# Expert outputs of the second layer's first step: four groups summed on VectorE, and the token sums as one fp32r pass

## The chip, the cores and the metric

The kernel runs on one core of one Trainium2 chip. The metric is device time in microseconds (us). One execution also has a hardware profile; its rows are what this document reads. The engines are TensorE (PE, with its weight loads as PEld), VectorE (DVE), ScalarE (ACT), GpSimd (POOL) and the queue of SyncE (SPq), which issues most DMAs.

## The reference

Two layers over 8 batches of 512 tokens and 256 channels. The part that matters is the hand-over between them: the mixture of 32 experts of the first layer is added back to the tokens, and this sum opens the second layer.

```python
# first layer, experts choose tokens (b = 8, E = 32, K = 8, s = 512)
vals_t, idx_t = jax.lax.top_k(probs.transpose(0, 2, 1), K)
...
h = jax.nn.gelu(h, approximate=False)
o = jnp.einsum('bej,ejo->beo', jnp.concatenate([h, ones], -1), w2)
out_tok = jnp.einsum('beo,bke->bkeo', o, vals).reshape(b, K * E, d)
out = jnp.zeros_like(x).at[jnp.arange(b)[:, None], flat_idx].add(out_tok)
...
x = x + _L0_attn_ref(xn, ...) + _L0_ffn_ref(xn, ...)
xn = _layernorm(x, axis=-1)
x = x + _L1_attn_ref(xn, ...) + _L1_ffn_ref(xn, ...)
```

The scatter-add is written as a matrix product. For a batch, `pick` (32 experts x 512 tokens) holds the weight with which an expert's output goes to a token, and `out = pick^T o`.

## The kernel before

`attend` is the first layer. It runs NTURN = 64 turns (8 batches x 8 head pairs), and beside the attention it computes one of the 32 experts every two turns. An expert's hidden units are cut into GRP = 4 groups, and each group's share of the output stays apart: the DRAM tensor `eo_d` holds, for each expert, 4 x 32 rows (group, batch slot) of 256 channels. `second_layer` follows in the same program. It holds one function for each engine, and each engine works through its own instructions in the order in which they are written; semaphores (`Signal`) tie the engines together, and `wait_ge` holds back everything behind it on its engine.

The tensor instructions of the second layer run as `first()` for batch 0, then `turn(b)` for b = 0 to 6, then `last(7)`. `turn(b)` does the products of batch b and, between them, the opening steps of batch b + 1:

- `add(b+1)` (L1547): the token sums. Four matmuls 128x128 by 128x256, plain fp32, write the added expert outputs of 512 tokens into the banks `bF`. All four groups are in the contraction: the 128 rows of `pick4` are `pick` four times over, and the 128 rows of `eo` are 4 groups x 32 experts. Each fp32 matmul has two records in the trace.
- `memory(b)`, `up(b, ...)` (L1581, L1600), `down(b, ...)` (L1611, L1617): the products of batch b, all of them pairs of high and low fp32r parts (hi x lo, lo x hi, hi x hi).
- `turn_x(b+1)` (L1557) transposes the normalised tokens, `router(b+1)` (L1565) and `turn_shut(b+1)` (L1572) do the routing of the second layer.

In `first()` the order is `add(0)`, two quarters of the last output projection of the first layer (`output`, L972), `turn_x(0)`, a third quarter, `router(0)`, the fourth quarter, `turn_shut(0)`. `add(0)` stands right behind the last `values` (L928) of the first layer.

On VectorE `front(0)` opens the second layer: `norm(0)` adds the residual to the banks (L1707), takes the statistics (L1712, L1715, L1717), waits for GpSimd's power (L1698) and writes the normalised tokens (L1721); later come `split`, `choose` and `copy_shut` (L1760). What stands ahead of it on VectorE is the last low part of the attention output, `yT_lo` (L1297). In `turn(b)` the order ends with `copy_shut(b+1)` and `finish(b)` (L1776, two halves, one for each half of `down`), and the next turn begins with `norm`.

On SyncE `get_x` loads the tokens and four copies of `pick` (L1514, L1516), `get_eo` the expert outputs (L1520); both for batch b + 2 as soon as `add` and the residual sum of batch b + 1 are done (`free`). The tiles `eo` and `pick4` have one buffer each.

```python
for j in range(GRP):
    eng.dma_start(eo[j * E:(j + 1) * E, :], eo_d[:, j * E + b, :]).then_inc(load.sem, load.unit)
...
def add(b):
    eng.wait_ge(load.sem, load.at(b))
    eng.wait_ge(lo_done.sem, lo_done.at(b - 1))
    eng.wait_ge(shutT_done.sem, shutT_done.at(b - 1))
```

Of the kernel before, what the change touches and what calls it, by code (L numbers as in the profile page):

```python
# [7 lines left out]
F32 = mybir.dt.float32  # L8
F32R = mybir.dt.float32r
# [591 lines left out]
def attend(nc, t, out, g):  # L601
# [18 lines left out]
    with ExitStack() as ctx:  # L620
# [10 lines left out]
        qkn = sq  # L631
        slope32 = sb("slope32", [P, NT, 2])
        shift32 = sb("shift32", [P, NT, 2])
        qT_hi, qT_lo = sb("qT_hi", [P, T], F32R), sb("qT_lo", [P, T], F32R)
        kT_hi, kT_lo = sb("kT_hi", [P, T], F32R), sb("kT_lo", [P, T], F32R)
        routed, scores, hidden, early = share(
            nc, ctx, "area_p", routing_tiles(g),
            tuple((f"prob{u}{h}", [P, off[NT]], F32) for u in range(2) for h in range(2)) + (
# [100 lines left out]
        def filled(n):  # L739
# [5 lines left out]
        jobs_at.update({(NTURN, 0): (8, 9), (NTURN, 1): (10, 11)})  # L745

        second = second_layer(nc, t, out, dict(
            g, ctx=ctx, up_hi=up_hi, up_lo=up_lo, downT_hi=downT_hi, downT_lo=downT_lo, readT_hi=readT_hi, readT_lo=readT_lo,
            spread=spread, shutT=shutT, rT=rT, number=number, area_raw=area_raw, area_sq=area_sq, hidden=hidden,
            hT=hidden["hT"], area_w1=area_w1, area_w2=area_w2, bF=bS[1:3], bR=bS[0], bU=bQ, bD=bR[0:2], bMem=bR[2],  # L750
            x1_stored=xr_store, prepared=prepared))
# [1 line left out]
        with nc.Block() as block:  # L753
            @block.sync
            def _(eng):
                def load_xT(b):
                    eng.wait_ge(pe_q.sem, pe_q.at((b - 1) * HP - 1))
                    eng.dma_start(xT_hi[:, b % 2, :, :].bitcast(F32), xnT_hi_d[b]).then_inc(xT_load[b % 2].sem, 16)
                    eng.dma_start(xT_lo[:, b % 2, :, :].bitcast(F32), xnT_lo_d[b]).then_inc(xT_load[b % 2].sem, 16)

                def load_w1(m):
                    eng.wait_ge(pe_h.sem, pe_h.at(m - 1))
                    eng.dma_start(w1[:, :, :], t["L0_ffn_w1"][m, 0:C, :].rearrange("(k p) f -> p k f", p=P)).then_inc(w1_load.sem, 16)
                    eng.wait_ge(biased.sem, biased.at(m - 1))
                    for j in range(GRP):
                        eng.dma_start(bias1[j * E:(j + 1) * E, :], t["L0_ffn_w1"][m, C, j * FW:(j + 1) * FW].partition_broadcast(E)).then_inc(
                            bias1_load.sem, 16)

                def load_w2(m):
                    eng.wait_ge(pe_eo.sem, pe_eo.at(m - 1))  # L770
                    eng.dma_start(w2[:, :, :], t["L0_ffn_w2"][m, 0:F, :].rearrange("(j p) c -> p j c", p=P)).then_inc(w2_load.sem, 16)
                    eng.wait_ge(eo_done.sem, eo_done.at(m - 1))
                    eng.dma_start(bias2[0:E, :], t["L0_ffn_w2"][m, F, :].partition_broadcast(E)).then_inc(bias2_load.sem, 16)

                def store_eo(m):
                    eng.wait_ge(eo_done.sem, eo_done.at(m))
                    eng.dma_start(eo_d[m], eo).then_inc(eo_store.sem, 16)
                route.sync(eng)
                route.over(eng)
                load_w1(0)  # L780
                load_w2(0)
                eng.dma_start(proj_in[:, :, :], t["L0_attn_Wproj"].rearrange("(h p) c -> p h c", p=P)).then_inc(wp_load.sem, 16)
                eng.dma_start(g["rb"][:], t["L1_ffn_router_b"].partition_broadcast(P)).then_inc(g["l1_load"], 16)
                eng.dma_start(g["backT"][g["M1"]:g["M1"] + 1, :], t["L1_ffn_b2"].unsqueeze(0)).then_inc(g["l1_load"], 16)
                with nc.allow_non_contiguous_dma(reason="1024 biases, once"):
                    eng.dma_start(g["b1"][:, :], t["L1_ffn_b1"].rearrange("(h p) -> p h", p=P)).then_inc(g["l1_load"], 16)

                for s in range(NTURN + 1):
                    b = s // HP
                    if begins_in(s) is not None and begins_in(s) + 1 < E:  # L790
                        load_w1(begins_in(s) + 1)
                    if s % HP == 1:
                        eng.wait_ge(xr_store.sem, xr_store.at(b - 1))
                        eng.dma_start(xr[:, :, :], t["L0_attn_x"][b].rearrange("(n p) c -> p n c", p=P)).then_inc(xr_load.sem, 16)
                    if s % HP == HP - 2 and b + 2 < B:
                        load_xT(b + 2)
                    if s == NTURN - 1:
                        eng.wait_ge(squared.sem, squared.at(s))
                        eng.wait_ge(norm_done.sem, norm_done.at(s))
                        eng.wait_ge(gate_in.sem, gate_in.at(s))  # L800
                        eng.wait_ge(v_done.sem, v_done.at(s))
                        second.get_x(eng, 0)
                    if s == NTURN - HP - 1:
                        eng.wait_ge(pe_q.sem, pe_q.at(NTURN - HP - 1))
                        for i in range(2):
                            eng.dma_start(w1n[i][:, :, :], t["L1_ffn_w1"][i * 4 * P:(i + 1) * 4 * P, :].rearrange(
                                "(h p) c -> p h c", p=P)).then_inc(w1n_load.sem, 16)
                    if s == NTURN - 2:
                        eng.wait_ge(pe_h.sem, pe_h.at(E - 1))
                        eng.dma_start(w2n[:, :, :], t["L1_ffn_w2"].rearrange("(k p) f -> p k f", p=P)).then_inc(w2n_load.sem, 16)  # L810
                    if ends_in(s) is not None:
                        store_eo(ends_in(s))
                        if ends_in(s) + 1 < E:
                            load_w2(ends_in(s) + 1)
                    if s == NTURN - 1:
                        eng.wait_ge(pe_eo.sem, pe_eo.at(E - 1))
                        for dst, src in ((rn, t["L1_ffn_router_w"]), (m1n, t["L1_attn_W1"]),
                                         (m2n[:, :, :], t["L1_attn_W2"].rearrange("(k p) m -> p k m", p=P)),
                                         (wk[:, :, :], t["L1_attn_W_K"].rearrange("(k p) c -> p k c", p=P))):
                            eng.dma_start(dst, src).then_inc(small_load.sem, 16)  # L820
                    if s > 0 and s % HP == 0:
                        if s == NTURN:
                            eng.wait_ge(eo_store.sem, eo_store.at(E - 1))
                            second.get_eo(eng, 0)
                            second.free(eng, 0)
                            second.get_x(eng, 1)
                            second.get_eo(eng, 1)
                        eng.wait_ge(o_done.sem, o_done.at(b - 1))
                        eng.dma_start(x1_d[b - 1].rearrange("(n p) c -> p n c", p=P), xr[:, :, :]).then_inc(xr_store.sem, 16)
                eng.wait_ge(g["l1_load"], 3 * 16)  # L830
                second.sync(eng)
# [626 lines left out]
def second_layer(nc, t, out, g):  # L1458
# [13 lines left out]
    xo = area[:, N:2 * N].rearrange("p (n c) -> p n c", n=NT)  # L1472
    pick4 = area[:, 2 * N:2 * N + T]
    eo = area[:, 2 * N + T:2 * N + T + C]
    area = g["area_w1"]
    x1 = area[:, :].rearrange("p (u n c) -> p u n c", u=2, n=NT)
    area = g["area_w2"]
# [19 lines left out]
    shut = piece(NT * NB).rearrange("p (n i) -> p n i", n=NT)  # L1497

    ev = lambda name, per, unit=1: Signal(ctx, nc, name, per, unit)
    load, store = ev("load3", 2 * GRP + 1, 16), ev("store3", 1, 16)  # L1500
    pe_add, pe_xT, pe_r, pe_shut = ev("pe_add", 2), ev("pe_xT3", 2), ev("pe_r", 1), ev("pe_shut", 1)
    pe_mem, pe_up, pe_down = ev("pe_mem", 1), ev("pe_up", HC), ev("pe_down", 2)
# [14 lines left out]

    def get_eo(eng, b):
        for j in range(GRP):
            eng.dma_start(eo[j * E:(j + 1) * E, :], eo_d[:, j * E + b, :]).then_inc(load.sem, load.unit)  # L1520

    def free(eng, b):
        eng.wait_ge(pe_add.sem, pe_add.at(b))
# [16 lines left out]
    def tensor(eng, output):  # L1540

        def add(b):
            eng.wait_ge(load.sem, load.at(b))
            eng.wait_ge(lo_done.sem, lo_done.at(b - 1))
            eng.wait_ge(shutT_done.sem, shutT_done.at(b - 1))
            for n in range(NT):
                m = eng.matmul(bF[n // 2][:, (n % 2) * C:(n % 2 + 1) * C], pick4[:, n * P:(n + 1) * P], eo[:, :],  # L1547
                               start=True, stop=True)
                if n % 2:
                    m.then_inc(pe_add.sem, pe_add.unit)  # L1550
# [102 lines left out]

    def scalar(eng):

        def copy_x(b):
            eng.wait_ge(hi_done.sem, hi_done.at(b - 1))
            eng.wait_ge(lo_done.sem, lo_done.at(b - 1))
# [17 lines left out]
        def turn(b):  # L1676
            memory(b)
            relu(b, range(0, 3))
            copy_x(b + 1)
            relu(b, range(3, HC))  # L1680

        def last(b):
            memory(b)
            relu(b, range(HC))
        copy_x(0)
        for b in range(B - 1):
            turn(b)
        last(B - 1)
# [9 lines left out]
            eng.tensor_tensor(rstd[:, :], var[:, :], half[:, 0:NT], ALU.pow).then_inc(rstd_done.sem, rstd_done.unit)  # L1698

    def vector(eng, output):  # L1700

        def norm(b):
            eng.wait_ge(load.sem, load.at(b))
# [74 lines left out]
                    x1[:, b % 2, 2 * i:2 * i + 2, :], ALU.add).then_inc(out_done.sem, out_done.unit)  # L1778

        def front(b):  # L1780
            norm(b)
            output(0)
            output(1)
# [2 lines left out]
            choose(b)  # L1786
            output(3)
            copy_shut(b)

        def turn(b):  # L1790
            norm(b + 1)
# [3 lines left out]
            choose(b + 1)  # L1795
            relu_low(b, range(6, HC))
            copy_shut(b + 1)
            finish(b)

        def last(b):  # L1800
# [29 lines left out]
```

## Time and profile before

| what | value |
|---|---|
| median of 3 runs | 1371.68 us (1370.08 to 1376.79) |
| the profiled execution's own time | 1374.09 us |
| its span in the profile | 1372.4 us |
| mean granted TensorE clock | 0.983 of full speed |
| PE busy | 1321.2 us, 96% of the span |
| DVE busy | 1057.4 us, 77% |
| ACT busy | 938.2 us, 68% |
| POOL busy | 194.8 us, 14% |
| second layer (first `add` to the last output) | 1097.7 to about 1372 us |

Times of rows are microseconds from the start of the span, unless a row says ns. The profiled execution took 1.7 us more than its span, and 2.4 us more than the median. "PEclk" in rows is the clock that TensorE was granted, as a share of its full 2.4 GHz; 0.50 is 1.2 GHz.

### The profile page before, as it was taken

Reading aid. Unit: us, or ns where it says so; the run is one execution under the profiler, and the core shown is the slowest. Engines: PE = TensorE matmul, PEld = TensorE weight load, DVE = VectorE, ACT = ScalarE, POOL = GpSimd, SP = SyncE. Lnnn points to the kernel's source line nnn. Section 1 sums busy time; section 2 is a strip of 40 time slices with the busy share of each in tenths; the row PEclk is TensorE's granted clock in tenths of the full one; section 3 lists DMA queues with packets and bytes.
Section 4 is the critical chain, followed back from the end, with each engine's and each line's share of the span. In section 5 each row is a group of like instructions: output and inputs, shape, how many; then the busy total and the mean of one; then the engine's idle time right before and its main releaser. Section 6 shows DMA issues by size and latency. Waiting matters only on the chain.

```text
span 1372.4 us, 31987 instructions
## 1 busy us (share of the span) xinstructions
PE 1321.2 (96%) x11472; PEld 1114.1 (81%) x11472; DVE 1057.4 (77%) x3292; ACT 938.2 (68%) x2357; POOL 194.8 (14%) x564
## 2 busy tenths in 40 slices
PE   4989999999999999999999999999999799999998
PEld 2678888888888888888888888878887588999897
DVE  6869996999699699969996996999699665544542
ACT  5759885888588588858886895988588433333333
POOL 4612111111011111111110111111111100000000
PEclk8699999999999999999999999999999899999999
DMA  5552241323233232413232332223132221111100
GB/s 209 189 167 87 73 136 54 119 101 100 73 102 107 75 98 74 134 57 117 101 106 67 106 103 83 91 83 126 65 109 67 79 70 43 43 43 43 43 16 31
DMA packets 88335, 123.15 MB, mean 90 GB/s; under 512 B 8577, under 2 KB 74482, under 8 KB 88178
## 3 DMA queue, kind: packets, MB, share of 16 engines
q1 hardware_dynamic: 87858, 121.11, 27.6%
q8 instruction: 92, 1.51, 0.5%
q14 instruction: 65, 0.53, 0.1%
q10 hardware_dynamic: 320, 0.00, 0.0%
HBM read 101.69 MB, written 19.40 MB: 88 GB/s over the span
## 4 chain that ended last, share of the span: by engine, by line
PE 76%; ACT 13%; DVE 4%; issue 2%; DMA 0%; POOL 0%; SPq 0%; ACTq 0%; DVEq 0%; POOLq 0%
PE at L848 15%; PE at L861 9%; PE at L900 8%; PE at L928 8%; PE at L1581 7%; PE at L972 7%; PE at L1617 7%; ACT prob L1114 5%; PE at L881 2%; PE at L939 2%; PE at L892 2%; ACT probT L1123 1%; PE at L886 1%; ACT area_raw L1071 1%; ACT L1133 1%
## 5 line engine op out<-in xcount | busy, mean ns | idle before, releaser
L1114 ACT ACTIVATE prob<-prob,low 128x512 f32<-128x512 f32 (+3 forms) x512 | 280.8, 551 | 115.9 <-DVE low L1268 115.9
L1268 DVE CUSTOM_DVE_ANT_0 prob<-at,mask 128x512 f32<-128x512 f32 (+3 forms) x512 | 219.8, 485 | 9.8 <-PE at L861 9.8
L848 PE MATMUL at<-w_hi,c_lo 128*128 128x386 f32 x512 | 189.9, 371 | 1.5 <-DVE area_raw L1213 1.5
L848 PE MATMUL at<-w_lo,c_hi 128*128 128x386 f32 x512 | 174.0, 340 | 0.0
L848 PE MATMUL at<-w_hi,c_hi 128*128 128x386 f32 x512 | 173.8, 340 | 0.0
L1281 DVE TENSOR_SCALAR prob<-prob,rec 128x512 f32<-128x512 f32 (+3 forms) x512 | 169.4, 395 | 4.5
L900 PE MATMUL at<-ident,prob 128*128 128x128 f32 x1280 | 165.6, 276 | 3.1 <-DVE low L1268 1.8
L928 PE MATMUL at<-probT,v 128*32 128x512 f32 (+3 forms) x2048 | 152.9, 439 | 4.6 <-DVE probT L1291 2.8
L900 PEld LDWEIGHTS at<-ident,prob 128*128 128x128 f32 x1280 | 143.5, 142 | 10.6 <-DVE yT_lo L1297 1.6
L928 PEld LDWEIGHTS at<-probT,v 128*32 128x32 f32 x2048 | 68.2, 110 | 90.5 <-issue 81.8
L1123 ACT ACTIVATE probT<-at 128x512 f32<-128x512 f32 (+1 forms) x256 | 130.3, 536 | 5.3 <-PE at L900 2.7
L1401 POOL TENSOR_TENSOR slope<-gl,omega 128x8 f32<-128x8 f32 x64 | 12.8, 200 | 836.7 <-DVE gl L1242 836.7
L1071 ACT ACTIVATE area_raw<-at 128x386 f32<-128x386 f32 x192 | 93.5, 487 | 19.8 <-PE at L848 18.1
L848 PEld LDWEIGHTS at<-w_hi,c_lo 128*128 128x128 f32 x512 | 97.0, 189 | 2.2 <-DVE area_raw L1213 1.9
L848 PEld LDWEIGHTS at<-w_lo,c_hi 128*128 128x128 f32 x512 | 97.3, 190 | 0.0
L1114 ACT ACTIVATION_READ_ACCUMULATOR prob<-prob,low 128x1 f32 x512 | 96.8, 189 | 0.0
L848 PEld LDWEIGHTS at<-w_hi,c_hi 128*128 128x128 f32 x512 | 96.7, 189 | 0.1
L861 PE MATMUL at<-kT_hi,qT_hi 64*128 64x512 f32 (+3 forms) x512 | 86.5, 332 | 6.6 <-ACT kT_hi L1101 6.6
L861 PE MATMUL at<-kT_lo,qT_hi 64*128 64x512 f32 (+3 forms) x512 | 84.9, 325 | 1.5
L861 PE MATMUL at<-kT_hi,qT_lo 64*128 64x512 f32 (+3 forms) x512 | 84.6, 324 | 0.0
L1667 ACT ACTIVATE mem<-at 64x512 f32<-64x512 f32 x8 | 4.8, 594 | 116.0 <-PE at L1581 116.0
L861 PE MATMUL at<-kaug,qaug 64*128 64x512 f32 (+3 forms) x512 | 83.2, 319 | 0.0
(225 smaller groups left out, 3243.5 us busy)
## 6 DMA issues: line engine op xcount, KB each, us to landing
area_w<-in_L_ffn_w SPq DMA_DIRECT2D x65, 1024.0 KB, 5.7
bias<-in_L_ffn_w SPq DMA_DIRECT2D x160, 32.0 KB, 4.5
x_in<-in_L_attn_x SPq DMA_DIRECT2D x8, 512.0 KB, 5.5
xr<-in_L_attn_x SPq DMA_DIRECT2D x8, 512.0 KB, 4.9
eo_d<-hidT SPq DMA_DIRECT2D x32, 128.0 KB, 1.8
x_d<-xr SPq DMA_DIRECT2D x8, 512.0 KB, 3.0
area_raw<-x_d SPq DMA_DIRECT2D x8, 512.0 KB, 3.9
out<-area_raw SPq DMA_DIRECT2D x8, 512.0 KB, 2.9
```

Of the source, the lines that this page charges most:

```text
L848: m = eng.matmul(bQ[n % 2][:, 0:W], a[:, (j // HP) % 2, k, n * P:(n + 1) * P], w[:, k, j % HP, :], start=start, stop=(k == KC - 1 and a is ...
L861: m = eng.matmul(bC[i][:, at:at + (c + 1) * P], q[rows, c * P:(c + 1) * P], k[rows, 0:(c + 1) * P], start=ready is k_hi_done, stop=q is qaug)
L900: m = eng.transpose(bP[h][i][:, at:at + P], prob[s % 2][h][:, off[c] + kc * P:off[c] + (kc + 1) * P], ident[:, :])
L928: m = eng.matmul(bY[rows, kc * P:T], v[:, s % 2, kc, rows], probT[j * E // D][:, offT[kc]:offT[kc + 1]], start=(kc == 0), stop=(kc == NT - 1))
L972: m = eng.matmul(bQ[n % 2][:, 0:C], y[:, h, n * P:(n + 1) * P], w[:, h, :], start=(h == 0 and y is yT_lo), stop=(h == HP - 1 and y is yT_h ...
L1071: eng.activation(raw[:, j % 2, n, :], bQ[n % 2][:, 0:W], ACT.Copy).then_inc(raw_A.sem, 1)
L1114: eng.activation(sl, sl, ACT.Exp, scale=-1.0, bias=low[:, i:i + 1], accum_out=den[:, i:i + 1]).then_inc(exp_done.sem, 1)
L1123: eng.activation(probT[h][:, x:y], bP[h][i][:, 0:y - x], ACT.Copy).then_inc(done.sem, 1)
L1268: eng.tensor_tensor_reduce(out=prob[s % 2][h][:, off[c]:off[c + 1]], in0=bC[i][:, at:at + (c + 1) * P], in1=mask[:, (NT - 1 - c) * P:T], s ...
L1281: p = eng.tensor_scalar(sl, sl, rec[:, k:k + 1], None, ALU.mult)
L1581: m = eng.matmul(bank[:, :], w[:, k, :], x[:, b % 2, k, :], start=start, stop=(k == KC - 1 and w is hi and x is xT_hi))
L1617: m = eng.matmul(o, part[:, h, n * P:(n + 1) * P], w[:, h, :], start=False, stop=(h == HC - 1 and part is hT_hi and w is downT_hi))
```

## The change

The four groups are no longer summed by the contraction. `get_eo` loads all four groups of every expert into each of four blocks of 32 rows (a new tile `eo4`, 128 x 4 x 256), and a reduction on VectorE sums them, so that every block holds the same 32 summed outputs. The contraction's 128 rows then carry the high and low parts instead: `eo_s` is high, low, high, low by blocks of 32 rows, and `pick_s` is high, high, low, low. One fp32r matmul over 128 rows gives all four partial products. ScalarE rounds `pick4` to its high part (`high_pick`), VectorE does the reduction and the rest (`split_eo`). The new tiles lie over `qT_hi`, `qT_lo`, `kT_hi` and `kT_lo` of the first layer, for which SyncE waits for the last scores before its first `get_eo`.

```diff
@@ attend
-        qT_hi, qT_lo = sb("qT_hi", [P, T], F32R), sb("qT_lo", [P, T], F32R)
-        kT_hi, kT_lo = sb("kT_hi", [P, T], F32R), sb("kT_lo", [P, T], F32R)
+        turned, added = share(
+            nc, ctx, "area_q", tuple((n, [P, T], F32R) for n in ("qT_hi", "qT_lo", "kT_hi", "kT_lo")),
+            (("eo4", [P, GRP, C], F32), ("pick_s", [P, T], F32R), ("eo_s", [P, C], F32R)))
...
                         if s == NTURN:
                             eng.wait_ge(eo_store.sem, eo_store.at(E - 1))
+                            eng.wait_ge(pe_s.sem, pe_s.at(NTURN - 1))
                             second.get_eo(eng, 0)
...
     def get_eo(eng, b):
         for j in range(GRP):
-            eng.dma_start(eo[j * E:(j + 1) * E, :], eo_d[:, j * E + b, :]).then_inc(load.sem, load.unit)
+            eng.dma_start(eo4[j * E:(j + 1) * E, :, :], eo_d.rearrange("e (j i) c -> i e j c", j=GRP)[b]).then_inc(load.sem, load.unit)
...
         def add(b):
-            eng.wait_ge(load.sem, load.at(b))
+            eng.wait_ge(eo_split.sem, eo_split.at(b))
...
-                m = eng.matmul(bF[n // 2][:, (n % 2) * C:(n % 2 + 1) * C], pick4[:, n * P:(n + 1) * P], eo[:, :],
+                m = eng.matmul(bF[n // 2][:, (n % 2) * C:(n % 2 + 1) * C], pick_s[:, n * P:(n + 1) * P], eo_s[:, :],
                                start=True, stop=True)
...
     def scalar(eng):
+        def high_pick(b):
+            eng.wait_ge(load.sem, load.at(b))
+            eng.wait_ge(pe_add.sem, pe_add.at(b - 1))
+            eng.activation(pick_s[:, :], pick4[:, :], ACT.Copy).then_inc(pick_hi.sem, pick_hi.unit)
...
             relu(b, range(3, HC))
+            if b + 2 < B:
+                high_pick(b + 2)
...
+        high_pick(0)
         copy_x(0)
+        high_pick(1)
...
     def vector(eng, output):
+        def split_eo(b):
+            eng.wait_ge(load.sem, load.at(b))
+            eng.wait_ge(pe_add.sem, pe_add.at(b - 1))
+            eng.tensor_reduce(eo[:, :], eo4[:, :, :].rearrange("p j c -> p c j"), AX.X, ALU.add).then_inc(eo_sum.sem, eo_sum.unit)
+            eng.wait_ge(eo_sum.sem, eo_sum.at(b))
+            eng.tensor_copy(eo_s[:, :], eo[:, :]).then_inc(eo_hi.sem, eo_hi.unit)
+            eng.wait_ge(eo_hi.sem, eo_hi.at(b))
+            for j in (1, 3):
+                rows = slice(j * E, (j + 1) * E)
+                eng.tensor_tensor(eo_s[rows, :], eo[rows, :], eo_s[rows, :].bitcast(F32), ALU.subtract).then_inc(eo_split.sem, eo_split.unit)
+            eng.wait_ge(pick_hi.sem, pick_hi.at(b))
+            eng.tensor_tensor(pick_s[2 * E:P, :], pick4[2 * E:P, :], pick_s[2 * E:P, :].bitcast(F32), ALU.subtract).then_inc(
+                eo_split.sem, eo_split.unit)
...
         def front(b):
+            split_eo(b)
             norm(b)
...
             copy_shut(b)
+            split_eo(b + 1)
 
         def turn(b):
...
             copy_shut(b + 1)
+            if b + 2 < B:
+                split_eo(b + 2)
             finish(b)
```

VectorE's order where the second layer begins, before (`area_w<-at,area_raw` is the residual sum of `norm`, the tiles of the second layer are slices of `area_raw`, `area_w` and `area_sq`):

```order
L1291 COPY probT<-at 128x384
L1297 TENSOR_TENSOR yT_lo<-at,yT_hi 128x512
L1707 TENSOR_TENSOR area_w<-at,area_raw 128x512 x2
L1712 BN_STATS area_sq<-area_w 128x6 x4
L1715 BN_AGGR area_sq<-area_sq 128x2 x4
L1717 TENSOR_SCALAR area_sq<-area_sq 128x4
L1721 TENSOR_SCALAR area_w<-area_w,area_sq 128x256 x4
```

The same place after the change, with batch 0's reduction (`eo` is `eo4`, `area_raw` here the summed outputs, then `pick4`):

```order
L1294 COPY probT<-at 128x384
L1300 TENSOR_TENSOR yT_lo<-at,yT_hi 128x512
L1719 TENSOR_REDUCE area_raw<-eo 128x256
L1721 CAST eo_s<-area_raw 128x256
L1725 TENSOR_TENSOR eo_s<-area_raw,eo_s 32x256 x2
L1727 TENSOR_TENSOR pick_s<-area_raw,pick_s 64x512
L1735 TENSOR_TENSOR area_w<-at,area_raw 128x512 x2
L1740 BN_STATS area_sq<-area_w 128x6 x4
```

Five instructions stand between the last `yT_lo` of the first layer and the first `norm`; batch 1's five stand in the same way between `copy_shut(0)` and `norm(1)`.

VectorE's order at the end of a turn, before (`shutT` is `copy_shut`, `area_raw<-at,area_w` the two halves of `finish`):

```order
L1755 TENSOR_SCALAR area_sq<-area_sq 128x64
L1769 TENSOR_TENSOR hT_lo<-hT,hT_hi 128x512 x2
L1760 CAST shutT<-at 16x512
L1776 TENSOR_TENSOR area_raw<-at,area_w 128x512 x2
L1707 TENSOR_TENSOR area_w<-at,area_raw 128x512 x2
L1712 BN_STATS area_sq<-area_w 128x6 x4
```

The same place after the change:

```order
L1783 TENSOR_SCALAR area_sq<-area_sq 128x64
L1797 TENSOR_TENSOR hT_lo<-hT,hT_hi 128x512 x2
L1788 CAST shutT<-at 16x512
L1719 TENSOR_REDUCE area_raw<-eo 128x256
L1721 CAST eo_s<-area_raw 128x256
L1725 TENSOR_TENSOR eo_s<-area_raw,eo_s 32x256 x2
L1727 TENSOR_TENSOR pick_s<-area_raw,pick_s 64x512
L1804 TENSOR_TENSOR area_raw<-at,area_w 128x512 x2
L1735 TENSOR_TENSOR area_w<-at,area_raw 128x512 x2
```

In turns 0 to 5 the five instructions of batch b + 2 stand between `copy_shut(b+1)` and `finish(b)`. On TensorE nothing moves; its eight `add` have four records each instead of eight.

## Rows read from the trace of the kernel before

**Rows 1.** The page, busy time of each engine over the span.

```profile
PE 1321.2 (96%) x11472; PEld 1114.1 (81%) x11472; DVE 1057.4 (77%) x3292; ACT 938.2 (68%) x2357; POOL 194.8 (14%) x564
```

**Rows 2.** Stretches: each engine's busy us, then PEclk, DMA share, GB/s.

```profile
1115.20:1147.50 32.30, 32.30 (x203) 28.97 (x204) 15.72 (x44) 11.72 (x19) 1.01 (x1) 1.00 0.15 45
```

**Rows 3.** The chain that ended last, one turn: start us, us, what.

```profile
1147.57 1.73 PE at L1547 x8
...
1176.94 2.84 PE at L1617 x24
1179.78 1.73 PE at L1547 x8
```

**Rows 4.** The same chain where the second layer begins.

```profile
1097.78 1.92 PE at L1547 x8
1099.70 5.67 PE at L972 x48
...
1113.78 0.52 PE at L1572 x4
1114.33 0.69 DVE shutT L1760
1115.15 1.97 PE at L1547 x8
```

**Rows 5.** VectorE in order of time, there: start, us, what, [idle before].

```profile
1098.63 0.69 DVE L1297 TENSOR_TENSOR yT_lo<-at,yT_hi 128x512 fp32r<-128x512 f32 x1 [5.64 <-ACT yT_hi L1128]
1099.24 1.28 DVE L1707 TENSOR_TENSOR area_w<-at,area_raw 128x512 f32<-128x512 f32 x2
```

**Rows 6.** VectorE's groups by shape: count, busy us, mean ns, idle before.

```profile
L1217 DVE TENSOR_REDUCE ssq<-area_sq 128x16 f32<-128x1024 f32 x64 | 77.8, 1215 | 4.8 <-ACT area_sq L1078 4.8
...
L1769 DVE TENSOR_TENSOR hT_lo<-hT,hT_hi 128x512 fp32r<-128x512 f32 x64 | 44.2, 691 | 35.4 <-ACT hT_hi L1674 34.4
...
L1313 DVE TENSOR_TENSOR hidT<-at,bias 128x256 f32<-128x256 f32 x32 | 13.4, 418 | 4.0 <-PE at L956 4.0
...
L1727 DVE CAST c_hi<-area_w 128x1024 fp32r<-128x1024 f32 x8 | 5.6, 694 | 2.7 <-ACT area_w L1662 2.7
```

**Rows 7.** DMA: first loads of the experts' outputs on SyncE's queue.

```profile
1084.35 1.85 SPq L1520 DMA_DIRECT2D area_raw<-eo_d  x4
1100.59 0.38 SPq L1514 DMA_DIRECT2D area_raw<-x_d  x1
```

**Rows 8.** The page, DMA issues: count, KB each, median us to landing.

```profile
area_raw<-x_d SPq DMA_DIRECT2D x8, 512.0 KB, 3.9
```

**Rows 9.** Stretches around two idle times of TensorE; columns of Rows 2.

```profile
81.10:82.90 1.80, 0.00 (x0) 0.00 (x0) 1.70 (x6) 0.85 (x3) 0.00 (x0) 1.00 0.91 330
83.60:86.90 3.30, 3.10 (x14) 2.61 (x13) 1.35 (x2) 1.88 (x3) 1.53 (x7) 0.50 1.02 330
1084.60:1086.80 2.20, 0.00 (x0) 0.00 (x0) 0.00 (x0) 0.41 (x1) 0.00 (x0) 1.00 0.67 184
1087.10:1097.20 10.10, 8.66 (x47) 5.43 (x50) 2.99 (x9) 1.37 (x3) 1.04 (x2) 0.50 0.00 1
1097.40:1114.20 16.80, 16.80 (x144) 15.96 (x136) 11.14 (x39) 2.97 (x4) 1.04 (x1) 1.00 0.19 57
```

**Rows 10.** VectorE from the end of one turn into the next.

```profile
1173.28 0.68 DVE L1760 CAST shutT<-at 16x512 fp32r<-16x512 f32 x1 [4.91 <-PE at L1572]
1173.89 0.67 DVE L1776 TENSOR_TENSOR area_raw<-at,area_w 128x512 f32<-128x512 f32 x1
1179.82 0.69 DVE L1776 TENSOR_TENSOR area_raw<-at,area_w 128x512 f32<-128x512 f32 x1 [5.26 <-PE at L1617]
1180.78 1.46 DVE L1707 TENSOR_TENSOR area_w<-at,area_raw 128x512 f32<-128x512 f32 x2 [0.27 <-PE at L1547]
...
1185.42 1.38 DVE L1721 TENSOR_SCALAR area_w<-area_w,area_sq 128x256 f32<-128x256 f32 x4 [1.12 <-POOL area_sq L1698]
```

**Rows 11.** TensorE's weight loads in that turn, where the next batch's transposes begin.

```profile
1187.37 1.02 PEld L1557 LDWEIGHTS at<-ident,area_w 128*128 128x128 f32 x8
```

More of the change, by code:

```diff
@@ L633, in attend @@
         shift32 = sb("shift32", [P, NT, 2])
-        qT_hi, qT_lo = sb("qT_hi", [P, T], F32R), sb("qT_lo", [P, T], F32R)
-        kT_hi, kT_lo = sb("kT_hi", [P, T], F32R), sb("kT_lo", [P, T], F32R)
+        turned, added = share(
+            nc, ctx, "area_q", tuple((n, [P, T], F32R) for n in ("qT_hi", "qT_lo", "kT_hi", "kT_lo")),
+            (("eo4", [P, GRP, C], F32), ("pick_s", [P, T], F32R), ("eo_s", [P, C], F32R)))
+        qT_hi, qT_lo, kT_hi, kT_lo = (turned[n] for n in ("qT_hi", "qT_lo", "kT_hi", "kT_lo"))
         routed, scores, hidden, early = share(
@@ L747, in attend @@
         second = second_layer(nc, t, out, dict(
-            g, ctx=ctx, up_hi=up_hi, up_lo=up_lo, downT_hi=downT_hi, downT_lo=downT_lo, readT_hi=readT_hi, readT_lo=readT_lo,
+            g, ctx=ctx, added=added, up_hi=up_hi, up_lo=up_lo, downT_hi=downT_hi, downT_lo=downT_lo, readT_hi=readT_hi, readT_lo=readT_lo,
             spread=spread, shutT=shutT, rT=rT, number=number, area_raw=area_raw, area_sq=area_sq, hidden=hidden,
@@ L1474, in second_layer @@
     eo = area[:, 2 * N + T:2 * N + T + C]
+    eo4, pick_s, eo_s = (g["added"][k] for k in ("eo4", "pick_s", "eo_s"))
     area = g["area_w1"]
@@ L1499, in second_layer @@
     ev = lambda name, per, unit=1: Signal(ctx, nc, name, per, unit)
+    pick_hi, eo_sum, eo_hi, eo_split = ev("pick_hi", 1), ev("eo_sum", 1), ev("eo_hi", 1), ev("eo_split", 3)
     load, store = ev("load3", 2 * GRP + 1, 16), ev("store3", 1, 16)
```

## Prediction

> **What bounds the kernel now.** I read the page first: TensorE is busy for 96% of the span, VectorE for 77% [rows 1]. That is a mean over the whole program, and the change touches only the second layer, so I then asked for one stretch of it: from 1115.2 to 1147.5 TensorE is busy for all of 32.3 us at full clock, VectorE for 15.7, ScalarE for 11.7 [rows 2]. The chain that ended last says the same: from one `add` to the next, 1147.57 to 1179.78, it is TensorE from end to end, 32.2 us a turn [rows 3]. Seven such turns follow each other. In a turn, then, what TensorE saves counts in full until some other engine is late. The opening of the layer is different. There the chain goes from `add(0)` through the output projection to `turn_shut(0)`, and then leaves TensorE for the copy on VectorE, on which `add(1)` waits [rows 4]. At this place time added on VectorE is time added to the kernel.
>
> **What the cheaper matmuls save.** An `add` takes 1.73 us in a turn [rows 3]. Its successor is four fp32r matmuls of the same size, 128x128 by 128x256, as `down` has them; 24 of those take 2.84 us, 0.118 us each [rows 3], so four take 0.47. The saving is 1.26 us for each `add`, eight times: 10.1 us, if nothing else moved.
>
> **What the split costs on VectorE.** Five instructions for each batch. The reduction reads 1024 elements a row and the nearest row is a reduction of that size, 1.215 us. Subtractions: 0.69 us at 512 columns, 0.42 at 256 [rows 6]; the number of rows in use (32 or 64 here) should not matter, since the columns are what is streamed. These two give 0.145 us fixed and 1.07 ns a column. The cast is faster per column: 0.694 us at 1024, so (0.694 - 0.145) / 1024 = 0.54 ns, and 0.28 us at 256 columns. Together 1.215 + 0.28 + 0.42 + 0.42 + 0.69 = 3.0 us. Neighbours overlap a little (the next instruction starts 0.61 us after one of 0.69 [rows 5]), and those that wait for a result do not; I leave the sum at 3.0. Its lower bound is 2.8, with every overlap counted.
>
> The reduction's reads are not like those of the row. The summed index is the outer one of `eo4`, so neighbours in reading order lie 1 KB apart; the row's reduction reads contiguous elements. No row of this trace has such a read on VectorE. Bounds: not under 1.2 us, and I take twice that, 2.4 us, as the upper end. I take the lower value, since the row is the same operation on as many elements.
> The Trainium skill (SBUF - State Buffer, Door 1: The DMA port swizzle) says that an access which leaves the 16-byte line it was on pays a penalty; here that would be every access. It gives no figure for VectorE, and no run here shows it; it is the rival C below.
>
> ScalarE's copy of `pick4` (512 columns; I bound it by VectorE's 0.69 us for as many [rows 6]) is hidden: at the opening it runs while VectorE sums, and in a turn ScalarE is busy for 11.7 of 32.3 us [rows 2]. What is queued behind it there is the memory's activation of the next batch, which needs TensorE's results of the next turn.
>
> **Where the split falls, at the opening.** The first split stands behind `yT_lo` on VectorE. Its data are there early: the first expert loads were issued at 1084.35 to 1086.2 [rows 7], and even 512 KB, which it now is, lands in some 4 us [rows 8], before 1091. VectorE sits idle for 5.64 us before `yT_lo` [rows 5], but the split may not use it: it comes behind in the order. It begins at 1099.24, where `norm` began [rows 5], and ends at 1102.2. `add(0)` waits for it with the whole of TensorE behind it. The semaphore costs 0.1 to 0.15 (the copy ends at 1115.02, `add(1)` starts at 1115.15 [rows 4]), and an `add` after an idle time takes 0.24 more than one in the stream (1.97 against 1.73 [rows 3, 4]). So `add(0)` starts at 1102.4 instead of 1097.78, and the projection at 1102.4 + 0.47 + 0.24 = 1103.1 instead of 1099.70: **+3.4 us**. The saving of 1.26 is already in this.
>
> The second split stands between `copy_shut(0)` and `norm(1)`, and `add(1)` waits for it. Before, `add(1)` began at 1115.15; now it begins 2.9 us later relative to the copy, and takes 1.26 less: **+1.65 us**. Its data: the loads for batch 1 are issued once the residual sum of batch 0 is done, at 1100.59 before [rows 7], about 1104.6 now; the queue takes some 5 us for nine issues, and landing takes 4 more, so all is there at about 1114. The copy now ends after 1118. This is hidden.
>
> **The clock.** TensorE will be idle from 1097.8 to 1102.4, 4.6 us, and again for 0.9 + 2.9 = 3.8 us before `add(1)`. The trace of before shows what shorter gaps do: after a gap of at least 1.8 us at 81 and one of at least 2.2 us at 1084.6 the granted clock is 0.50, that is 1.2 GHz, and stays there while TensorE works again; in the first case to 86.9, about 4 us after work came back, in the second to 1097.2, over 10 us after [rows 9]. At half clock a microsecond of work takes two, so the price of a gap is half of that time: 2.0 us, or 5.2. Behind both new gaps TensorE has dense work (16.8 busy of 16.8 us, and 32.3 of 32.3 [rows 2, 9]), as behind the first of the two, while in the second case it was busy for 8.66 of 10.1 us [rows 9]. I take 2.0 us for each: **+4.0 us**. Lower bound 0, upper 10.4 for both.
>
> **Where it falls in the turns.** Six splits (batches 2 to 7) stand between `copy_shut` and `finish`. There VectorE has idle time: the copy starts at 1173.28, the first half of `finish` needs 0.67 us, the second waits until 1179.82 after 5.26 us of idleness [rows 10]. The 3.0 us fit into the 5.26. The loads were issued at the start of that turn, over 15 us earlier. So the six cost nothing themselves; without that cover each would cost 3.0.
>
> But something else becomes late. `norm` gives `turn_x` its input. It ends at 1185.42 + 1.38 = 1186.80 [rows 10], and TensorE comes for it at 1187.37 [rows 11], a slack of 0.57 us. With the shorter `add` TensorE comes at 1187.37 - 1.26 = 1186.11. `norm` gets earlier too, but less: its first sum starts right behind `finish`, at 1179.82 + 0.61 = 1180.43 instead of 1180.78, and its second no longer waits for the second half of `add`, so the pair takes 1.28 us [rows 5] instead of 1.46 [rows 10]. It ends 0.53 earlier, at 1186.27. With 0.13 for the semaphore TensorE waits for 0.3 us. A turn saves 1.26 - 0.3 = 0.97 us, six turns **-5.8 us**. Bounds: 0.8 if the sums keep their pace, 1.26 if the wait does not come, so -4.8 to -7.6.
>
> **The sum.** 3.4 + 1.65 + 4.0 - 5.8 = +3.25 us on the profiled execution's 1374.09 (span 1372.4 and 1.7 around it), 1377.3; it lay 2.4 us over the median of the runs, so against the median of 1371.68 I expect 1375. At full clock the sum would be -0.75: what the turns give back, the two waits at the opening take. Of two medians of this kernel about 0.5%, 6.9 us, can be told from no change (its three runs lie 6.7 us apart).
>
> **The rivals.**
> A, the forecast: two gaps, each with about 4 us at 1.2 GHz, six turns that gain a microsecond. 1375, own range 1372 to 1378. Chance 0.55.
> B, the clock costs less than I think: it falls after one gap only or after neither, or was at 1.2 GHz up to 1097 anyway [rows 9] and the gap changes little. Then -0.75 to +1.25: 1371 to 1373. For it: only two gaps of this kind are shown [rows 9]; against it: both new gaps are longer than these. Chance 0.18.
> C, the strided reduction takes 2.4 us. Then both opening waits grow by 1.2, +2.4: 1377.5. In the turns 4.2 + 0.67 us still fit between 1173.89 and 1179.82. It would cost there only if the reduction took over 2.2 us more than I count. Chance 0.1.
> D, slower beyond doubt: the clock stays at 1.2 GHz for 10.4 us of work behind each gap, as it did once before 1097.2 [rows 9]. 3.4 + 1.65 + 10.4 - 5.8 = +9.65: 1381.3. It decides when the low stretches behind the gaps come to more than 15 us together (5.05 - 5.8 + 7.6 = 6.9). For it, the longest case in the trace; against it, the dense work behind both gaps. Chance 0.1.
> E, the turns give nothing: the new matmul is not one pass, or `norm` is later than worked out. Then +9: 1380.7. Against it, the 24 matmuls of the same kind at 0.118 us each [rows 3]. Chance 0.05.
> F, the waits at the opening are far shorter than 3 us each, and the turns give the full 1.26: -7 or so, 1365. The order on VectorE speaks against it. Chance 0.02.
>
> **How the numbers follow.** The time is A's. For the range I leave out most of D, E and F, and keep A, B, C: 1369.5 to 1380.5, with 1.5 us at each end for the scatter of a median. Slower by over 0.5% (over 1378.5) are D and E less their lower edges, and the upper edge of A and C: 0.13. Faster (under 1364.8) is F with some scatter: 0.03. Within 0.5%: 0.84.
>
> **What would show it.** Right: `add` with four records instead of eight; TensorE idle for about 4.6 us before `add(0)` and 3.8 before `add(1)`, both put down to VectorE's `pick_s`; a PEclk of 0.50 behind both; the reduction at 1.2 us; turns of 31.2 us instead of 32.2, with a short wait of the `turn_x` weight loads for `norm`. Wrong: turns that stay at 32.2, a reduction much over 1.2 us, no fall of the clock, or a low clock that lasts far beyond 4 us of work. The prediction would be wrong as a whole if VectorE ran late into `finish`, since then the six hidden splits would each cost time.

## The result: 0.4% slower, with the turns faster and the opening slower

| what | before | changed |
|---|---|---|
| median of 20 runs each | 1371.96 us (1369.82 to 1377.61) | 1377.68 us (1374.53 to 1381.82) |
| ratio to before | | 1.0038, 95% interval 1.0027 to 1.0049 |
| profiled execution, span | 1372.4 us | 1374.1 us |
| last `values` to last matmul, in the chain | 270.5 us | 274.5 us |

The last row is the one to compare by. The two spans differ by only 1.7 us, but in the profiled execution of the changed kernel the first layer, which the change does not touch but for the loads at its end, ended 2.3 us earlier (the last `values` end at 1095.5 instead of 1097.8). In the ten profiles of this case that point lies anywhere between 1093.9 and 1099.0, so this is scatter. From that point on the second layer takes 4.1 us more. The ratio of the runs, 1.0038, is 5.2 us (3.7 to 6.7).

The page of the changed kernel, busy time of each engine; TensorE lost 11.7 us against [rows 1], VectorE gained 29.7:

```profile
PE 1309.5 (95%) x11440; PEld 1103.1 (80%) x11440; DVE 1087.1 (79%) x3332; ACT 941.3 (69%) x2365; POOL 194.5 (14%) x564
```

The chain that ended last in the changed kernel, where the second layer begins, with start and length in us; it answers to [rows 4]:

```profile
1091.28 4.23 PE at L931 x32
...
1096.93 1.89 DVE area_raw L1719
...
1100.06 0.70 DVE pick_s L1727
...
1100.81 1.22 PE at L1552 x4
1102.03 7.19 PE at L975 x48
...
1117.55 0.52 PE at L1577 x4
...
1118.70 1.87 DVE area_raw L1719
...
1121.83 0.70 DVE pick_s L1727
...
1122.62 1.19 PE at L1552 x4
```

The reader is to see two places at which the chain leaves TensorE for five instructions of VectorE. TensorE stands still from 1095.51 to 1100.81, 5.3 us, and from 1118.07 to 1122.62, 4.55 us, where it was 0.85 before. VectorE in order of time, from the last `yT_lo` to the first `norm`, answers to [rows 5]:

```profile
1096.32 0.69 DVE L1300 TENSOR_TENSOR yT_lo<-at,yT_hi 128x512 fp32r<-128x512 f32 x1 [5.67 <-ACT yT_hi L1131]
1096.93 1.88 DVE L1719 TENSOR_REDUCE area_raw<-eo 128x256 f32<-128x1024 f32 x1
1098.84 0.29 DVE L1721 CAST eo_s<-area_raw 128x256 fp32r<-128x256 f32 x1
1099.16 0.87 DVE L1725 TENSOR_TENSOR eo_s<-area_raw,eo_s 32x256 fp32r<-32x256 f32 x2
1100.06 0.69 DVE L1727 TENSOR_TENSOR pick_s<-area_raw,pick_s 64x512 fp32r<-64x512 f32 x1
```

The split takes 3.8 us, and 1.88 of them are the reduction. The 5.67 us of idleness ahead of `yT_lo` stay unused. Then the clock, by stretches (columns of [rows 2]):

```profile
1095.60:1098.00 2.40, 0.00 (x0) 0.00 (x0) 1.68 (x2) 1.10 (x2) 0.00 (x0) 1.00 0.00 0
1098.10:1100.70 2.60, 0.00 (x0) 0.00 (x0) 2.47 (x5) 0.00 (x0) 0.00 (x0) 0.56 0.00 0
1100.90:1104.70 3.80, 3.80 (x18) 3.80 (x19) 2.90 (x9) 0.00 (x0) 0.00 (x0) 0.50 0.07 19
1105.00:1118.00 13.00, 13.00 (x111) 12.62 (x109) 7.45 (x28) 3.00 (x4) 1.04 (x1) 0.99 0.35 93
...
1122.00:1122.60 0.60, 0.00 (x0) 0.02 (x1) 0.51 (x1) 0.00 (x0) 0.00 (x0) 0.77 0.00 0
1122.70:1125.20 2.50, 2.50 (x8) 2.21 (x9) 1.65 (x4) 0.00 (x0) 0.00 (x0) 0.50 0.00 0
1126.00:1155.00 29.00, 29.00 (x189) 26.14 (x188) 17.03 (x44) 12.22 (x20) 1.01 (x1) 1.00 0.18 46
```

Within each idle time the granted clock falls from 1.00 to 0.50, 1.2 GHz: on the way through the first (the mean of its second half is 0.56), only near the end of the second (0.77 over its last stretch). It stays there for some 4 us of work behind the first and about 3 behind the second. The first two quarters of the projection take 7.19 us instead of 5.67 for it.

In the turns the chain shows the gain (the counterpart of [rows 3]):

```profile
1183.58 2.85 PE at L1622 x24
1186.43 0.47 PE at L1552 x4
...
1193.13 0.03 issue
1193.16 1.09 PE at L1562 x8
...
1217.67 0.47 PE at L1552 x4
```

An `add` is 0.47 us, and a turn 1217.67 - 1186.43 = 31.24 us instead of 32.21. The new wait is there too, at the transposes of the next batch: TensorE's weight loads stood still until VectorE had the normalised tokens.

```profile
1193.16 0.86 PEld L1562 LDWEIGHTS at<-ident,area_w 128*128 128x128 f32 x8 [0.46 <-DVE area_w L1749]
```

And VectorE at the end of a turn, the counterpart of [rows 10]: split and first half of `finish` end at 1216.46, and 1.25 us remain of the 5.26 of idleness before the second half.

```profile
1211.17 0.68 DVE L1788 CAST shutT<-at 16x512 fp32r<-16x512 f32 x1 [4.91 <-PE at L1577]
1211.78 2.00 DVE L1719 TENSOR_REDUCE area_raw<-eo 128x256 f32<-128x1024 f32 x1
...
1217.71 0.69 DVE L1804 TENSOR_TENSOR area_raw<-at,area_w 128x512 f32<-128x512 f32 x1 [1.25 <-PE at L1622]
1218.49 1.29 DVE L1735 TENSOR_TENSOR area_w<-at,area_raw 128x512 f32<-128x512 f32 x2
```

### The profile page after: what moved, and what is told of

It is laid out like the page before. It is cut to its first block, busy times and chain, and to the rows that moved or that the text cites. A ratio compares the mean times of both kernels' runs of the same rounds, so it can differ in the third digit from the quotient of the medians.

```text
span 1374.1 us, 31988 instructions
## 1 busy us (share of the span) xinstructions
PE 1309.5 (95%) x11440; PEld 1103.1 (80%) x11440; DVE 1087.1 (79%) x3332; ACT 941.3 (69%) x2365; POOL 194.5 (14%) x564
## 4 chain that ended last, share of the span: by engine, by line
PE 75%; ACT 14%; DVE 5%; issue 2%; DMA 0%; POOL 0%; SPq 0%; ACTq 0%; DVEq 0%; POOLq 0%
PE at L851 15%; PE at L864 9%; PE at L931 8%; PE at L903 8%; PE at L1586 7%; PE at L975 7%; PE at L1622 7%; ACT prob L1117 5%; PE at L884 2%; PE at L942 2%; ACT probT L1126 2%; PE at L895 2%; ACT area_raw L1074 1%; PE at L889 1%; ACT L1136 1%
## 5 line engine op out<-in xcount | busy, mean ns | idle before, releaser
L1220 DVE TENSOR_REDUCE ssq<-area_sq 128x16 f32<-128x1024 f32 x64 | 77.8, 1216 | 4.8 <-ACT area_sq L1081 4.8
```

## The experiments

The theory: two waits for the split at the opening, a clock that falls in each, and six turns that gain a microsecond each. Its rivals: the larger loads or VectorE's extra work cost time in the turns; the clock costs nothing; the strided read is not what makes the reduction long. Ratios are to the kernel before, timed on the same chip; the changed kernel's is 1.0038. The first five kernels were run 12 times each, the last three 6 times. "Length" is that of the second layer in the one profiled execution of each, from the last `values` to the last matmul: 270.5 us before, 274.5 changed.

| kernel | ratio (95% interval) | length |
|---|---|---|
| batch 0's split earlier | 0.9991 (0.9977 to 1.0004) | 268.7 |
| contiguous reads in the reduction | 1.0027 (1.0013 to 1.0042) | 272.8 |
| idle times filled with matmuls | 1.0010 (0.9997 to 1.0023) | 271.8 |
| old `add` for batches 0 and 1 | 0.9965 (0.9951 to 0.9979) | 264.7 |
| two adds for the reduction | 1.0011 (1.0001 to 1.0022) | 272.7 |
| both splits hidden | 0.9951 (0.9931 to 0.9970) | 263.5 |
| the same, transposes later | 0.9946 (0.9926 to 0.9966) | 261.6 |
| reduction twice in the turns | 1.0064 (1.0048 to 1.0080) | 278.6 |

**Batch 0's split ahead of the last `yT_lo`.**

```diff
 # VectorE, attend, turn NTURN (ScalarE the same with high_pick(0))
+                    if s == NTURN:
+                        second.split_eo(eng, 0)
                     if s > 0:
                         copy_y(s - 1)
...
         def front(b):
-            split_eo(b)
             norm(b)
...
```

> Edit on the changed kernel: ScalarE's rounding of batch 0's choice and VectorE's split of batch 0 stand ahead of the last low part of the attention output instead of behind it. Theory of two waits: VectorE is idle there for 5.6 us, so the split (3.8 us) fits, add(0) follows the last values at once, TensorE's first idle time (5.3 us in the trace of the changed kernel) is gone and the clock does not fall there. What is left of the first wait is nothing, so this gives back 5.3 us plus half of the 4 us at 1.2 GHz behind it: some 7 us less than the changed kernel, 0.1 to 0.2% under the kernel before. The second wait (before add(1)) stays. Rival, the four times larger loads or the extra VectorE work in the turns are what costs: no change from the changed kernel's ratio of 1.004.

Length 268.7, so 5.8 us came back where 7 were expected; the ratio is 0.9991. In order of time on VectorE, the split now lies in the idle time, but begins only at 1093.20, behind other late work of the first layer, and ends 0.9 us after the `values`:

```profile
1092.73 0.55 DVE L1296 COPY probT<-at 128x384 f32<-128x384 f32 x1
1093.20 1.98 DVE L1538 TENSOR_REDUCE area_raw<-eo 128x256 f32<-128x1024 f32 x1
...
1096.44 0.69 DVE L1546 TENSOR_TENSOR pick_s<-area_raw,pick_s 64x512 fp32r<-64x512 f32 x1
1097.16 0.69 DVE L1302 TENSOR_TENSOR yT_lo<-at,yT_hi 128x512 fp32r<-128x512 f32 x1
```

So the wait shrank from 5.3 to 0.9 us with the same work on VectorE, and the projection ran in 5.92 us, at full clock. The place in the order made most of the first wait; that the amount of work counts too, as long as it stands there, is shown by the two shorter sums below. The wait of 0.9 us that is left accounts for most of the 1.2 us by which the expectation was missed.

**Contiguous reads.**

```diff
-            eng.tensor_reduce(eo[:, :], eo4[:, :, :].rearrange("p j c -> p c j"), AX.X, ALU.add).then_inc(eo_sum.sem, eo_sum.unit)
+            eng.tensor_reduce(eo[:, :], eo4[:, :, :].rearrange("p j c -> p (j c)").rearrange("p (c j) -> p c j", j=GRP), AX.X, ALU.add).then_inc(eo_sum.sem, eo_sum.unit)
```

> Edit on the changed kernel: the reduction reads its 1024 elements in the order in which they lie in the row, as 256 groups of 4 neighbours, so that the summed values are not the group sums that the reference needs; everything else is the same work. Theory that the 1 KB step between reads is what makes the reduction 1.88 us: it takes 1.2 us, both opening waits get 0.66 us shorter, 1.3 us less in all than the changed kernel. Rival, the reduction is slow for another reason (four inputs for each output, the larger output): it stays at 1.9 us and the time stays.

This kernel leaves out the sum over the groups and adds neighbours instead, so its output is not the reference's.

The reduction's own row: number, shortest, median and longest in ns.

```profile
L1719 DVE TENSOR_REDUCE area_raw<-eo x8: 1196/1196/1210, 1100.4 to 1307.3; 128x256 f32<-128x1024 f32 x8
```

1.20 us, where the changed kernel has 1860/2004/2004. Same count of inputs and outputs, so the step between reads is the cause. The length fell by 1.7 us, a little more than two times 0.66; most of the rest is a shorter time at 1.2 GHz behind the shorter first wait (the projection took 6.86 us instead of 7.19).

**Filled idle times.**

```diff
         def first():
+            eng.wait_ge(g["prep_last"][0], g["prep_last"][1])
+            warm(bU[1], 16)
             add(0)
...
             eng.wait_ge(prepared.sem, prepared.at(0))
+            warm(bMem, 14)
+        def warm(bank, n):
+            w = g["wp_hi"]
+            for _ in range(n):
+                eng.matmul(bank[:, :], w[:, 0, 0:P], w[:, 0:2, :].rearrange("p h c -> p (h c)"), start=True, stop=True)
...
```

> Edit on the changed kernel: TensorE fills the two idle times with matmuls on weights it has at hand, 16 of 128x128 by 128x512 before add(0) and 14 before add(1), results unused (3.6 and 3.2 us at full clock, less than either wait). Theory that the idle times cost clock: PEclk stays at 1.00 through the opening of the second layer and the kernel gains 1.7 us behind the first wait and 1.1 behind the second, 2.8 in all against the changed kernel (ratio 1.002). Rival, the clock behind the waits costs nothing that counts: the same ratio as the changed kernel, 1.004, or more if the filling runs over the waits.

```profile
1098.90:1102.40 3.50, 3.50 (x16) 2.81 (x16) 2.66 (x3) 1.12 (x2) 0.00 (x0) 1.00 0.00 0
1104.40:1117.00 12.60, 12.38 (x105) 12.18 (x106) 7.98 (x23) 3.00 (x4) 1.04 (x1) 1.00 0.39 106
1119.60:1123.00 3.40, 3.40 (x18) 2.67 (x16) 3.31 (x4) 0.00 (x0) 0.00 (x0) 1.00 0.45 154
1125.00:1150.00 25.00, 25.00 (x152) 21.89 (x151) 14.87 (x43) 12.21 (x20) 1.01 (x1) 1.00 0.23 53
```

PEclk is 1.00 in each of the four stretches. The useful work begins no earlier, since the split is as late as before (`add(0)` starts 5.5 us behind the last `values` instead of 5.3), and yet the length fell by 2.7 us and the ratio from 1.0038 to 1.0010. So the clock has a price of its own, 2.7 us here. It is less than the 3.5 us counted in the chain below, mostly because at full clock TensorE is early enough to meet another wait: its transposes now come right behind the last part of `norm(0)` in the chain, and take 1.10 us instead of 0.87.

```profile
1109.84 1.06 DVE area_w L1757 x3
1110.95 1.10 PE at L1562 x8
```

The Trainium skill (TensorE: Matmul & The Clock Gate, Why this matters for your kernels) advises against long idle gaps between bursts of matmuls for this reason; the trace agrees, with 0.50 behind both gaps.

**The old way for batches 0 and 1.**

```diff
         def add(b):
-            eng.wait_ge(eo_split.sem, eo_split.at(b))
+            old = b < 2
+            left, right = (pick4, eo) if old else (pick_s, eo_s)
+            if old:
+                eng.wait_ge(load.sem, load.at(b))
+            else:
+                eng.wait_ge(eo_split.sem, eo_split.at(b - 2))
...
```

The loads of batches 0 and 1 are the old ones too, and the first two roundings and splits are left out.

> Edit on the changed kernel: batches 0 and 1 are summed in the old way (four groups in a plain fp32 contraction, no split), batches 2 to 7 in the new way. Theory: the opening is as in the kernel before, and six turns take 31.24 instead of 32.21 us, 5.8 us less than the kernel before: ratio 0.996. Rival, the larger loads or VectorE's extra work slow the turns down or the saving of the turns is not real: ratio 1.000 or more.

```profile
1096.85 1.92 PE at L1560 x8
1098.77 5.67 PE at L975 x48
...
1146.74 0.47 PE at L1560 x4
...
1177.95 0.47 PE at L1560 x4
```

The opening is that of the kernel before (5.67 us for the projection's first half, no fall of the clock), the turns take 31.21 us, and the length is 264.7: 5.8 us less than before, the forecast of the turns to a tenth. This also settles the rival of the loads: from batch 2 on each expert load is four times as large here too, and costs nothing.

**Two adds for the reduction.**

```diff
-            eng.tensor_reduce(eo[:, :], eo4[:, :, :].rearrange("p j c -> p c j"), AX.X, ALU.add).then_inc(eo_sum.sem, eo_sum.unit)
+            eng.tensor_tensor(eo4[:, 0:2, :], eo4[:, 0:2, :], eo4[:, 2:4, :], ALU.add).then_inc(eo_pair.sem, eo_pair.unit)
+            eng.wait_ge(eo_pair.sem, eo_pair.at(b))
+            eng.tensor_tensor(eo[:, :], eo4[:, 0, :], eo4[:, 1, :], ALU.add).then_inc(eo_sum.sem, eo_sum.unit)
```

> Edit on the changed kernel: the strided reduction is replaced by two elementwise adds (512 columns, then 256), which read contiguous elements. Theory: 0.69 + 0.03 + 0.42 = 1.15 us instead of 1.88, so both opening waits are 0.75 us shorter, 1.5 us in all against the changed kernel; the turns stay at 31.24 us. Rival, that the reduction's length does not count because something else ends at the same time: no difference, the second layer as long as with the change (274.5 us from the last values to the last matmul).

```profile
1096.51 0.68 DVE L1720 TENSOR_TENSOR eo<-eo 128x512 f32<-128x512 f32 x1
1097.23 0.43 DVE L1722 TENSOR_TENSOR area_raw<-eo 128x256 f32<-128x256 f32 x1
```

The sum is ready 1.15 us after the split's start instead of 1.88. The length fell by 1.9 us for an expected 1.5; by the ratio, 1.0011, it is 3.7 us less than the changed kernel, but each of the two ratios is known only to 1.5 us, so the two figures agree. Two adds, which look like more work, are cheaper than one reduction with a large step.

**Both splits hidden.** Batch 0's split ahead of the last `yT_lo`, the two adds for the reduction, and in turn 0 the order below; ScalarE and VectorE take their work in turn 0 in the matching order:

```diff
         def turn(b):
-            add(b + 1)
-            memory(b)
-            up(b, range(0, 3))
-            turn_x(b + 1)
-            up(b, range(3, 6))
-            router(b + 1)
-            up(b, range(6, HC))
+            if b == 0:
+                memory(b)
+                up(b, range(0, 2))
+                add(b + 1)
+                up(b, range(2, 6))
+                turn_x(b + 1)
+                up(b, range(6, 7))
+                router(b + 1)
+                up(b, range(7, HC))
...
```

> Edit on the changed kernel: the split of batch 0 ahead of the last low part of the attention output, the two adds for the reduction, and in turn 0 TensorE does the memory product and two of the eight up products of batch 0 before add(1) (the transposes and the router of batch 1 come three products later; ScalarE and VectorE in the same order). Theory: both waits are gone and no clock falls, so all eight shorter adds count: from the last values to the last matmul 261 us against 270.4 in the kernel before, 9 us less, ratio 0.993. Rival, a gain of the turns alone, 5.7 us (ratio 0.9965), because the opening meets another wait.

Length 263.5 instead of the expected 261, ratio 0.9951. What TensorE waited for from 1088 us on (engine, releaser, total us, times, longest):

```profile
PE at L975 <- issue: 1.0, 1, 1.0
PE at L1612 <- DVE shutT L1807: 1.0, 1, 1.0
PE at L931 <- ACT probT L1126: 0.7, 1, 0.7
```

No wait for the split is left. Two of 1.0 us are, and I had left both out. For the first the view names no releaser, but VectorE's own row settles it:

```profile
1094.77 0.69 DVE L1302 TENSOR_TENSOR yT_lo<-at,yT_hi 128x512 fp32r<-128x512 f32 x1 [1.38 <-ACT yT_hi L1131]
```

`yT_lo` ends at 1095.46 and the projection, which reads it, starts at 1095.56; before, the 1.92 us of `add(0)` covered this. At the second, `memory(0)` waits for `copy_shut(0)` just as `add(1)` did in [rows 4]. They are 2.0 of the 2.5 us that are missing.

**The same, with the transposes one product later.**

```diff
-                up(b, range(0, 3))
+                up(b, range(0, 4))
                 turn_x(b + 1)
-                up(b, range(3, 6))
+                up(b, range(4, 6))
```

ScalarE and VectorE take their work in turns 1 to 6 in the matching order.

> The kernel of e6_both_hidden, and in turns 1 to 6 the transposes of the next batch come after four up products instead of three. Theory: TensorE's wait of 0.3 us for the normalised tokens, which is what keeps a turn at 31.24 instead of 30.95 us, is gone: 1.5 to 1.8 us less than e6_both_hidden, turns of 30.95 us, ratio 0.992. Rival: the wait is an artefact of how the records end, turns stay at 31.24 us.

```profile
1144.47 0.47 PE at L1578 x4
...
1152.75 0.87 PE at L1588 x8
...
1175.33 0.47 PE at L1578 x4
```

A turn is now 30.86 us, and the transposes 0.87 us as before the change. Length 261.6, 1.9 less, so the wait was real in the profile. By the runs' ratio the two kernels can't be told apart (0.9946 and 0.9951). These two are the fastest versions measured: 0.5% under the kernel before, 0.9% under the changed one.

**The reduction twice in the turns.**

```diff
+            if b >= 2:
+                eng.wait_ge(eo_sum.sem, eo_sum.at(b))
+                eng.tensor_reduce(eo[:, :], eo4[:, :, :].rearrange("p j c -> p c j"), AX.X, ALU.add).then_inc(eo_again.sem, eo_again.unit)
+                eng.wait_ge(eo_again.sem, eo_again.at(b - 2))
```

> Edit on the changed kernel: in batches 2 to 7 VectorE does the reduction a second time, with the same result. Theory of cover: 3.9 us of split and 0.67 of finish leave 1.25 us of idleness before the second half of finish, and 2.0 more overrun it by about 0.7 us, which comes out one for one at the transposes' wait: turns of 31.9 us instead of 31.24, 4 us more than the changed kernel in all, ratio 1.007. Rival, the cover is wider than the trace shows (TensorE's wait before the transposes absorbs it, or finish is not on the path): ratio as the changed kernel's, 1.004. Rival, every microsecond on VectorE counts in a turn: 12 us more.

```profile
1216.79 1.99 DVE L1723 TENSOR_REDUCE area_raw<-eo 128x256 f32<-128x1024 f32 x1
...
1220.04 0.69 DVE L1732 TENSOR_TENSOR pick_s<-area_raw,pick_s 64x512 fp32r<-64x512 f32 x1
1220.76 1.29 DVE L1809 TENSOR_TENSOR area_raw<-at,area_w 128x512 f32<-128x512 f32 x2
```

Both halves of `finish` now run back to back: the cover is used up. Length 278.6, 4.1 us more than with the change, 0.7 for each of six turns, where 2.0 us of work were added to each. So 1.3 us of it were free, which is the idle time that the trace of the changed kernel shows there (1.25).

## Why the prediction was right, step by step

The measured time, 1377.7, lies 2.7 us over the forecast of 1375 and inside its range, and forecast A held: two gaps, a clock that falls in both, six turns that gain a microsecond. But one of the signs that the prediction had named for being wrong came true as well, a reduction much over 1.2 us, and the measured time is nearer to rival C's 1377.5 than to A's 1375. So the mechanism was right and one of its costs was not. In the prediction's order:

**The saving of an add.** Forecast 0.47 us for four matmuls; measured 0.47.

**The split.** Forecast 3.0 us, measured 3.8. The cast (0.28; 0.29), the subtractions (0.42, 0.42 and 0.69; 0.87 for the pair, and 0.69) were right. The reduction was not: I took the lower end, 1.2 us, because the row was of the same operation and size; the contiguous variant has that figure, the real one 1.88. My upper end was 2.4, so rival C had the right mechanism at little more than half its price. The Trainium skill (SBUF — State Buffer, Door 1: The DMA port swizzle) says that an access which goes on to another 16-byte line pays a penalty; the trace agrees, with 1.86 to 2.00 us against 1.20.

**The opening.** Forecast +3.4 for the first wait and +1.65 for the second. In the chain the projection begins 6.52 us after the last `values` instead of 1.92, +4.6, of which 0.5 is an `add` at half clock (1.22 us instead of 0.71): +4.1. At the second the wait grew by 3.7 us less the 1.26 saved: +2.4. Both terms were mis-sized by 0.7 to 0.8 us, nearly all of it the reduction's extra 0.66 to 0.68.

**The clock.** Forecast +4.0, two gaps with 4 us each at 1.2 GHz. That the clock falls in both was right, and so was the first gap's length; behind the second it was low for less, and why it was is not shown. Counted in the chain it is 0.5 + 1.5 (projection) + 0.5 + 1.0 (`memory(0)`, 2.34 us instead of 1.38), 3.5 us; what filling the gaps gave back is 2.7. Rival D's 10 us of low clock did not come, in the profiled execution at least.

**The turns.** Forecast 31.24 us by a wait of 0.3 us for `norm`, -5.8 in six turns. Measured 31.24, and -5.8 in the experiment that changes the turns alone. That it fits to a hundredth is partly luck. The first sum of `norm` started 0.78 us behind the start of the last `finish`, not 0.61, so `norm` ended 0.35 us earlier in the turn, not 0.53, and the weight loads stood still for 0.46 us, not 0.3; but the turn lost only 0.29 us by it. The cover of the six splits held too, though with 1.25 us left where 2.3 were counted.

**The sum.** +4.1 + 2.4 + 3.5 - 5.9 = +4.1 us in the chain, forecast +3.25. The error, 0.8 us, is the 1.5 us by which the two waits were mis-sized, less half a microsecond of clock and 0.1 of the turns: errors that partly cancel. I gave 0.13 to a change clear of 0.5%, and the 0.38% measured lies below that.

What stays open: the ratio of the runs says 5.2 us (3.7 to 6.7), the profiled chain 4.1. Both agree within the interval, but a clock that stays low for longer in some executions would do the same, and one profile cannot show it.

## What to carry to other kernels

A step that is moved off the bound engine is free only where the engine that takes it over reaches it in time: here six of eight splits cost nothing, and the other two, with the clock behind them, made the opening some 10 us longer where six turns gave back 5.9. So look at the first and the last pass of a pipeline apart from its turns, ask what stands ahead of the new work in its engine's order, and put it where its data are ready, not where its result is used. Then count the wait behind it with the clock that it costs, and the wait that it was covering. And where groups lie far apart in a row, add slices elementwise before reaching for a reduction.

## What the runs showed of the hardware

- A VectorE reduction of 1024 fp32 elements to 256 takes 1.20 us with contiguous reads and 1.86 to 2.00 us when neighbouring reads lie 1 KB apart, half as much again and more. The difference between 1.86 and 2.00 goes with TensorE: in the profiles it was 1.86 to 1.88 us where TensorE stood still meanwhile (both waits of the changed kernel, the second wait with batch 0's split earlier), and 1.98 to 2.00 where it worked, in the turns and also at the opening once the idle times were filled with matmuls (2.00 and 1.98). Why was not tried.
- Two neighbouring subtractions on 32 rows each, with nothing to wait for between them, do not overlap (0.87 us for two of 0.42), while two of 128x512 do (1.29 for two of 0.69). The first pair starts on rows 32 and 96, the second on row 0 both times.
- TensorE's clock fell to 1.2 GHz within or at the end of the two idle times of 5.3 and 4.55 us (0.50 in the rows behind both). With 3.9 and 3.5 us of dummy matmuls in them it was granted 2.4 GHz throughout, in the one execution profiled.
